# Attention and block-quantised feed-forward layer: the division of the attention sums goes to GpSimd, bias and statistics are rearranged

## The reference

```python
xn = layernorm(x)                       # x: 16 batches x 512 tokens x 128
x  = x + attn(xn) + ffn(xn)
# attn: q = xn@Wqa@Wqb (16 heads of 8), k, v = xn@Wkva@Wkvb (4 heads); rope on q and k;
#       causal softmax(q k^T / sqrt(8)); o = w v; o @ Wout + bout
# ffn:  fp4_linear(silu(fp4_linear(xn, w_gate)) * fp4_linear(xn, w_up), w_down)   # 128 -> 352 -> 128
# fp4_linear quantises both operands in blocks of 16 before the product
```

## Time and profile before

| | us |
|---|---|
| median of 3 runs | 797.62 (795.21 to 798.21) |
| the profiled execution, its own time | 797.94 |
| its span, first to last instruction | 795.9 |
| outside the span | 2.0 |
| one step of the loop, T = 1 to 12 | 44.4 |
| granted TensorE clock, mean | 0.988 |

### The profile page before, as it was taken

The page is one execution under the profiler, slowest core; times in us unless marked ns, Lnnn a source line. Parts: engine busy times, 40 slices in busy tenths (PEclk is TensorE's granted clock), DMA queues, the critical chain, the costliest instruction groups (busy, mean ns, idle before and its releaser), DMA issues.

```text
span 795.9 us, 18365 instructions
## 1 busy us (share of the span) xinstructions
PE 722.8 (91%) x6453; PEld 442.3 (56%) x6453; DVE 644.0 (81%) x1390; ACT 535.1 (67%) x1154; POOL 612.3 (77%) x708
## 2 busy tenths in 40 slices
PE   2467889999999999999999999999999999998986
PEld 1233455665656565665656565565656665665434
DVE  6569788989888888989888988889888988878412
ACT  2213686867777777777776767777776867676672
POOL 5534597878889797878889797878889797856662
PEclk9998899999999999999999999999999999999998
DMA  4423233233334343243334343343434333341111
GB/s 113 115 68 88 73 86 102 86 108 110 96 92 116 104 118 96 89 117 98 103 99 119 88 116 96 91 115 96 108 99 116 87 117 93 93 102 38 56 49 35
DMA packets 85028, 75.48 MB, mean 95 GB/s; under 512 B 28642, under 2 KB 67010, under 8 KB 84938
## 3 DMA queue, kind: packets, MB, share of 16 engines
q1 hardware_dynamic: 84938, 74.32, 34.3%
HBM read 40.45 MB, written 27.25 MB: 85 GB/s over the span
## 4 chain that ended last, share of the span: by engine, by line
PE 39%; POOL 32%; ACT 11%; DVE 7%; issue 6%; DMA 3%; SPq 2%; POOLq 0%; DVEq 0%; ACTq 0%
PE pv_ps L1160 10%; POOL P L554 9%; PE exp_ps L1139 7%; POOL h L564 5%; PE max_ps L1124 5%; ACT P L961 5%; POOL h L567 5%; POOL h L570 4%; PE misc_ps L1184 3%; PE max_ps L1125 3%; PE misc_ps L1192 3%; DVE neg_max L737 3%; PE misc_ps L1209 3%; POOL q_split L645 2%; POOL rstd L596 2%
## 5 line engine op out<-in xcount | busy, mean ns | idle before, releaser
L737 DVE TENSOR_REDUCE neg_max<-max_ps 128x1 f32<-128x512 f32 (+3 forms) x768 | 429.9, 593 | 87.1 <-PE max_ps L1125 85.2
L961 ACT ACTIVATE P<-exp_ps 128x512 f32<-128x512 f32 x512 | 294.9, 599 | 167.7 <-PE exp_ps L1139 166.6
L1139 PE MATMUL exp_ps<-Q,K 128*128 128x512 bf16 (+3 forms) x1024 | 244.0, 301 | 10.3 <-ACT P L961 6.5
L1124 PE MATMUL max_ps<-K,Q 128*128 128x384 bf16 (+2 forms) x768 | 199.2, 278 | 18.9 <-DMA Kd<-K 11.7
L1125 PE MATMUL max_ps<-Kd,Q 128*128 128x128 bf16 x1024 | 191.3, 221 | 2.1 <-DVE neg_max L737 2.0
L554 POOL TENSOR_SCALAR_AFFINE_SELECT P<-P 128x512 f32<-128x512 f32 x256 | 161.8, 667 | 26.8 <-ACT P L964 26.8
L1160 PE MATMUL pv_ps<-P,V 128*32 128x512 f32 (+3 forms) x2048 | 163.9, 438 | 1.9 <-POOL P L554 0.8
L1124 PEld LDWEIGHTS max_ps<-K,Q 128*128 128x128 bf16 x768 | 75.9, 100 | 93.3 <-DVE neg_max L737 47.2
L1125 PEld LDWEIGHTS max_ps<-Kd,Q 128*128 128x128 bf16 x1024 | 98.4, 100 | 46.1 <-issue 22.7
L1139 PEld LDWEIGHTS exp_ps<-Q,K 128*128 128x128 bf16 x1024 | 79.7, 98 | 48.4 <-ACT P L961 27.1
L585 POOL TENSOR_TENSOR h<-gate_sb,up_half 128x352 f32<-128x352 f32 x64 | 59.6, 932 | 58.7 <-DVE gate_sb L750 58.6
(11 more groups left out here) (128 smaller groups left out, 974.1 us busy)
## 6 DMA issues: line engine op xcount, KB each, us to landing
Q<-q_scr SPq DMA_DIRECT2D x64, 224.0 KB
o_scr<-oT SPq DMA_DIRECT2D x31, 256.0 KB, 2.6
q_scr<-q_split SPq DMA_DIRECT2D x16, 384.0 KB, 2.6
Kd<-K SPq DMA_DIRECT2D x64, 96.0 KB
x_in<-x SPq DMA_DIRECT2D x16, 256.0 KB, 4.5
q_scr<-q_split SPq DMA_DIRECT2D x16, 256.0 KB, 2.9
x_res<-x SPq DMA_DIRECT2D x16, 256.0 KB, 5.7
out<-y SPq DMA_DIRECT2D x32, 128.0 KB, 4.3
```

What stands on the lines that cost most here:

```text
L737: nc.vector.tensor_reduce(neg_max[:, pr // 4, heads[0]:heads[0] + len(heads), pr % 4, i], max_ps[r % 3][:, 0:len(heads) * n].rearrange("p ...
L961: nc.scalar.activation(P[g % 2][:, hh + r % 2, col:col + 512], ps[:, :], ACT.Exp, scale=SCALE).then_inc(exp_done, 1)
L1124: nc.tensor.matmul(ps[:, col:col + d], Qt, Kt[:, half, g, 0:d], start=True, stop=True)
L1139: last = nc.tensor.matmul(exp_ps[n % 2][:, col:col + width], K[par][:, half, pr // 2, kb * 128:(kb + 1) * 128], Q[par][:, pr, kb * 128:S], ...
```

## The change

- `normalize` (the product `onT`) is issued by GpSimd, after `split_rest` and in front of `hidden(3)`, and no more by VectorE.
- `var_eps` is made on VectorE between tiles (3,4) and (3,5); `neg_mean` is gone, `shift` is one `scalar_tensor_tensor` on VectorE at the start of slot 5; GpSimd keeps `rstd`.
- v goes from PSUM straight to `V` by two VectorE copies, without `v_stage`; `V` has three buffers instead of two.
- The bias is row 96 of the third piece of `wdT`, against a row of ones in `hqT`; `x_bias` (GpSimd) is gone and y is made with `x_res`. The load of `x_res` for batch T-1 is issued at the start of step T instead of that for batch T.

```diff
-            (bout_sb[:, :], bout.partition_broadcast(128)),
+            (wdT[FC[2][1]:FC[2][1] + 1, 2, :], bout.unsqueeze(0)),
...
 # SP, start of a step
-                if T.has(0):
-                    T.wait(sp, x_bias_done, 1, 0, 0)
-                    sp.dma_start(x_res[:, :, :], x[T.batch(0)]...).then_inc(x_res_loaded, 16)
+                if T.has(-1):
+                    T.prev().misc_wait(sp, misc_read, "out1")
+                    sp.dma_start(x_res[:, :, :], x[T.batch(-1)]...).then_inc(x_res_loaded, 16)
...
 # POOL
-            def statistics(T):
-                T.wait(pool, mv_done, NT, 3, NT)
-                nc.gpsimd.tensor_scalar(var_eps[:, :], bn_mv[:, :, 1], EPS, None, ALU.add).then_inc(var_done, 1)
-                nc.gpsimd.tensor_scalar(neg_mean[:, :], bn_mv[:, :, 0], -1.0, None, ALU.mult).then_inc(var_done, 1)
-                T.wait(pool, var_done, 2, 3, 2)
+            def normalize(T):
+                T.wait(pool, o_loaded, 32, -1, 32)
+                T.wait(pool, o_inv_in, 32, -1, 32)
+                nc.gpsimd.tensor_tensor(onT[:, :], o_raw[:, :], o_spread[:, :], ALU.mult).then_inc(o_normed, 1)
+            def deviation(T):
+                T.wait(pool, var_done, 1, 3, 1)
                 nc.gpsimd.tensor_tensor(rstd[:, :], var_eps[:, :], half_neg[:, :], ALU.pow).then_inc(rstd_done, 1)
-                T.wait(pool, rstd_done, 2, 3, 1)
-                nc.gpsimd.tensor_tensor(shift[:, :], neg_mean[:, :], rstd[:, :], ALU.mult).then_inc(rstd_done, 1)
...
-                    for s in range(2):
-                        nc.gpsimd.tensor_copy(V[T.par(1)][...], v_stage[...]).then_inc(v_ready, 1)
...
-                statistics(T)
+                deviation(T)
                 split_rest(T, 1, 0)
+                normalize(T)
                 hidden(T, 3)
...
-                    nc.gpsimd.tensor_tensor(x_bias[:, :, :], x_res[:, :, :], bout_sb..., ALU.add).then_inc(x_bias_done, 1)
...
 # DVE
-                reduces(3, 4, 5)
+                reduces(3, 4)
+                if T.has(3):
+                    T.wait(dve, mv_done, NT, 3, NT)
+                    T.wait(dve, rstd_done, 2, 2, 1)
+                    nc.vector.tensor_scalar(var_eps[:, :], bn_mv[:, :, 1], EPS, None, ALU.add).then_inc(var_done, 1)
+                reduces(3, 5)
...
-                    nc.vector.tensor_copy(v_stage[:, :, :], misc_ps[1][:, 0:128]...).then_inc(misc_read[1], 1)
+                    for odd in range(2):
+                        nc.vector.tensor_copy(V[T.third(2)][:, :, odd::2, ...], misc_ps[1][:, 0:128]...)
...
-                reduces(5, 0)
-                normalize(T)
-                reduces(5, 1, 2)
+                if T.has(3):
+                    T.wait(dve, rstd_done, 2, 3, 1)
+                    nc.vector.scalar_tensor_tensor(shift[:, :], bn_mv[:, :, 0], -1.0, rstd[:, :], ALU.mult, ALU.mult)
+                reduces(5, 0, 1, 2)
```

More of the change, by code:

```diff
@@ L90, in batch, with third @@
         return self.t0 + off
+    def third(self, off):
+        return (self.t0 + off) % 3
     def wait(self, eng, sem, per, off, k):
@@ L191, in build @@
         Kd = sb("Kd", [128, 2, KVH, S], BF16)
-        V = [sb(f"V{i}", [128, NT, KVH, 32]) for i in range(2)]
+        V = [sb(f"V{i}", [128, NT, KVH, 32]) for i in range(3)]
         P = [sb(f"P{i}", [128, GH, P_WIDTH]) for i in range(2)]
@@ L534, in _ @@
             nc.gpsimd.memset(half_neg[:, :], -0.5).then_inc(consts_set, 1)
-            for i in range(2):
+            for i in range(3):
                 nc.gpsimd.memset(V[i][:, :, :, :], 0.0).then_inc(pool_const, 1)
@@ L539, in _ @@
             nc.gpsimd.memset(m_split[:, :, 64:128], 0.0).then_inc(pool_const, 1)
-            pool.wait_ge(pool_const, 5)
-            for i in range(2):
+            pool.wait_ge(pool_const, 6)
+            for i in range(3):
                 nc.gpsimd.memset(V[i][:, :, 0::2, 2 * D:2 * D + 1], 1.0).then_inc(pool_const, 1)
@@ L663, in iteration @@
                     quantize(T, 0, 3, *hs)
[L664 to L668, removed]
                 if T.has(3):
@@ L768, in invert @@
                 nc.vector.reciprocal(o_inv[:, g, :], o_sum[:, g, :]).then_inc(o_inv_done, 1)
[L770 to L776, removed]
-                    T.prev().misc_wait(dve, misc_filled, "out1")
-                nc.vector.tensor_tensor(onT[:, :], o_raw[:, :], o_spread[:, :], ALU.mult).then_inc(o_normed, 1)
             def output(T, n):
@@ L784, in output @@
                 if n == 0:
-                    T.wait(dve, x_bias_done, 1, -1, 1)
+                    T.wait(dve, x_res_loaded, 16, -1, 16)
                     T.wait(dve, stored, 32, -1, 0)
@@ L790, in output @@
                 nc.vector.tensor_tensor(y[:, c, :], misc_ps[0][:, 0:2 * E].rearrange("p (c e) -> p c e", c=2),
-                                        x_bias[:, c, :], ALU.add).then_inc(misc_read[0], 1)
+                                        x_res[:, c, :], ALU.add).then_inc(misc_read[0], 1)
             def finish(T):
@@ L813, in finish @@
                 T.wait(dve, stored, 32, -1, 0)
-                T.wait(dve, x_bias_done, 1, -1, 1)
+                T.wait(dve, x_res_loaded, 16, -1, 16)
                 for c, ps in enumerate(misc_ps + exp_ps):
                     dve.wait_ge(last_out, c + 1)
-                    nc.vector.tensor_tensor(y[:, c, :], ps[:, 0:E], x_bias[:, c, :], ALU.add).then_inc(last_y, 1)
+                    nc.vector.tensor_tensor(y[:, c, :], ps[:, 0:E], x_res[:, c, :], ALU.add).then_inc(last_y, 1)
             def iteration(T):
@@ L879, in iteration @@
                     T.wait(dve, x_loaded, 16, 3, 16)
-                    T.wait(dve, var_done, 2, 2, 2)
                     for c in range(NT):
@@ L910, in iteration @@
                     store_weights()
-                reduces(5, 0)
-                normalize(T)
-                reduces(5, 1, 2)
+                if T.has(3):
+                    T.wait(dve, rstd_done, 2, 3, 1)
+                    nc.vector.scalar_tensor_tensor(shift[:, :], bn_mv[:, :, 0], -1.0, rstd[:, :],
+                                                   ALU.mult, ALU.mult).then_inc(rstd_done, 1)
+                reduces(5, 0, 1, 2)
                 hidden_max(T, 3)
@@ L936, in iteration @@
                 reduces(7, 3, 4, 5)
+            nc.vector.memset(hqT[FC[2][1]:FC[2][1] + 1, 2, :], 1.0).then_inc(ones_row, 1)
             nc.vector.memset(last_sums[:, :, 0:HALF], 0.0).then_inc(dve_marks, 1)
@@ L1153, in weighted_sums @@
                     if g == 0:
-                        T.wait(pe, v_ready, 2, off, 2)
+                        T.wait(pe, v_ready, 1, off, 1)
+                        T.prev().prev().misc_wait(pe, misc_read, "v")
                 else:
@@ L1159, in weighted_sums @@
                     for j in range(GH):
-                        last = nc.tensor.matmul(pv_ps[32 * j:32 * j + 32, kb * 128:S], V[T.par(off)][:, kb, g, :],
+                        last = nc.tensor.matmul(pv_ps[32 * j:32 * j + 32, kb * 128:S], V[T.third(off)][:, kb, g, :],
                                                 P[g % 2][:, j, P_COL[kb]:P_COL[kb] + width],
```

34 lines of the change are left out of this document (17 added, 17 removed).

## The result

The changed kernel takes **790.12 us** (median of 6 runs, 788.24 to 792.68); the kernel before, beside it on the same chip, 795.8 (6 runs, 795.02 to 798.21). The ratio is 0.9926, interval 0.99 to 0.9953: 5.7 us less. The profiled execution of the changed kernel is the fastest of its six, 788.24 with a span of 785.8; the profiled one of before was with 797.94 at the upper end of its own (span 795.9). So the two traces differ by 10.1 us where the medians differ by 5.7. A later series of the changed kernel gave 791.1. Ratios leave out executions more than 1.5% above the fastest of their kernel; that is one, the 833.24 of experiment 5.

A forecast was written before the change was run, and what follows sets the result against it. A relay between TensorE with ScalarE and GpSimd bounds a middle step. Terms -3.6, -1.0, -2.6 and +1.65 make -5.55, from 797.9 to 792.4, written 792.2 for the median; own range 790.5 to 794.3, wide range 790 to 798.

The forecast's parts named there:

- T = 0: First step: no product there, so it keeps -1.03 from the statistics; TensorE's wait of 1.5 us leaves room.
- T = 13 and 14: GpSimd makes the product before L564 and TensorE no longer waits for onT: -1.3 each.
- T = 15: Late o_spread holds GpSimd's whole queue; L570 ends near 779.1 instead of 776.65: +1.65.
- Slot 7: Middle steps: without x_bias, x_scale falls by 0.61 and part of TensorE's 0.24 stall at tile (7,5) goes: -0.13.
- The run: GpSimd, T = 1 to 12: -1.03 statistics, +0.20 later hidden(3), -0.44 at L564; sum -0.24, taken as -0.17 a step.
- L564's relief: GpSimd's addition of h_mag, no longer beside onT on VectorE, gets shorter by 0.44 or a little less.
- holds GpSimd some 0.1: Before hidden(3): shift, if it waits for the product's end, gets in first and delays GpSimd; bounds 0 and 0.20.
- TensorE then has 0.27 - 0.1 in hand: At hqT0: the 0.27 wait less 0.1 for a late shift leaves TensorE 0.17, as much as GpSimd gains.
- rival D: Middle steps: shift not held, and VectorE 1.3 us lighter lets TensorE start slot 5 tiles earlier; 790.9, chance 0.10.
- A: Middle steps: L564 stays at 3.31 beside another VectorE instruction, product paid in full; step +0.07, 796.7, chance 0.15.
- B: End of slot 3: var_eps held behind q_split, up to 1.2 us; +0.1 to +0.3 a step, 798.3, chance 0.15.
- C: End of slot 3: var_eps held behind q_split, its price on the path, middle 0.8 a step; 805.5, slower, chance 0.10.

The follow-up runs named there:

- experiment 5: Kernel before with the statistics alone changed: var_eps and shift on VectorE, rstd left on GpSimd; 826.57 us, ratio 1.0349.
- number 10: Kernel before with the v copies alone: two VectorE copies from PSUM into a third buffer of V; 796.42 us, ratio 0.9992.
- number 12: The changed kernel once more, unaltered; 791.1 us, ratio 0.9917 against the kernel before.
- (3): Kernel before with the bias alone as a weight row and x_bias gone; 795.14 us, ratio 0.9973.
- (2): Kernel before with only the product onT moved to GpSimd, in front of hidden(3); 803.2 us, ratio 1.0071.
- (11): Changed kernel, all four statistics on GpSimd, var_eps and neg_mean ahead of q_split's third part except in T = -2; 795.3 us, ratio 0.9983.
- Number 8: Changed kernel with the product of T = 15 alone back on VectorE; 788.57 us, ratio 0.9899.
- (6): Changed kernel with var_eps one tile later, behind tile (3,5); 789.85 us, ratio 0.9911.

## Why the prediction came out as it did

Predicted 792.2, measured 790.12: faster as forecast, 2.1 us too high, inside the wide range of 790 to 798 but 0.4 below the forecast's own 790.5 to 794.3. By medians the gain is 5.7 us where the sum gave 5.55. The mechanism, a relay between TensorE and GpSimd in which GpSimd's run sets the step, is borne out. Two steps of the prediction failed: the level that the sum was taken from, and the size of the term for a middle step.

**The level.** The step is "It stands 0.3 above the median of the runs, so I write 792.2". That median was one of three runs, 797.62; with more of them it is 795.8 here and 796.6 to 797.0 in the three other series, and the profiled execution lies some 1 to 2 above. From 795.8 the same sum gives 790.25.

**The sum is right by parts that are not.** By the starts of `hqT0`, in us; the last column takes two other executions, number 10, whose steps are those of before, and number 12, the changed kernel again:

| part | predicted | before to changed | number 10 to 12 |
|---|---|---|---|
| T = 0 | -1.0 | -1.8 | -1.7 |
| T = 1 to 12 | -3.6 | -5.3 | -2.1 |
| T = 13 and 14 | -2.6 | -3.2 | -3.0 |
| T = 15 | +1.65 | +1.3 | +1.4 |
| from there to the end | 0 | -1.1 | +0.1 |
| sum | -5.55 | -10.1 | -5.2 |

- The term that was mis-sized is "12 x (-0.17 - 0.13) = -3.6": an undisturbed step gained 0.41, not 0.30, which makes -4.9.
- Slot 7, -0.13: measured -0.13 by itself (3).
- The run, -0.17: measured -0.27. The product, 1.23, and what left the run, 1.03, were right, and L564's relief too. What failed is "holds GpSimd some 0.1": a held `shift` takes nothing from `hidden(3)`, which starts 1.23 behind the product as if it were alone. Over twelve steps 1.2 us.
- "TensorE then has 0.27 - 0.1 in hand": had TensorE been 0.1 later, its wait for `h` would have ended with 0.17 of GpSimd's gain. It was 0.10 earlier: GpSimd gave 0.27 and a wait of 0.10 is left. I gave the product's departure from VectorE only the 0.18 of the wait; it is worth 0.35 (2), and the held `shift` costs back 0.1 to 0.2 (11). This was rival D's second half; D's first, that `shift` is not held, is wrong. The step is 0.41 shorter where I had 0.30 and D 0.42.
- T = 0: over four kernels with nearly this head it ends between 120.6 and 122.8, which I did not settle.
- T = 13 and 14: the waits for `onT`, 1.24 and 1.29, are gone, and the steps are 1.57 and 1.66 shorter. So "there is no wait for L570 to fall back on" held. In T = 14 `o_sum` lands late, VectorE waits 1.70 and 1.07, and the gain comes all the same.
- T = 15: GpSimd's idle time before the product is 1.42, not 1.9. Number 8 puts the net price of the new order there at 1.0.
- The last stretch had no term. 0.3 of it follows from T = 15's order; the rest, up to 0.75, goes with the granted clock of the last eight matmuls.
- Disturbed steps were in no term. They carry 0.6 us of the first trace of the changed kernel and 3.5 of the second, 2.9 of the 3.3 by which the two spans differ.

That the sum meets the difference of the medians is thus luck: the undisturbed steps, T = 0 and T = 13 and 14 gained 2.2 to 2.7 more than it had in these pairs, and disturbed steps, 2.6 more in number 12 than in number 10, can take as much back.

**The rivals.** A fell at once: L565 is 2.86 in every step. B was right in its mechanism and wrong as a state of every step: `var_eps` passes ahead by 0.27, I had 0.1 to 0.2, and is caught only where `o_sum` is late. Its price when it is caught in every step behind tile (3,5) is 0.05 (6), not the 0.1 to 0.3. Ahead of that tile, where the changed kernel has it, a caught `var_eps` comes with 0.64 for the step, near the 0.8 of C's middle. So C had a price that occurs, but in one to three steps of an execution and not in twelve; the late transfer has a share in the 0.64 that I did not part from it.

By the Trainium skill, SBUF - State Buffer, section "Who interferes with whom", the instruction that issues first has the shared ports for its whole length and the other blocks: "Issue order, not op shape, decides who blocks." The traces agree, with a number for each case: four elements take 0.16 us free and 1.13 behind `q_split`, 0.15 free and 0.67 behind the product; 512 elements take 1.31 behind the last piece of h and 2.82 behind the addition. By size alone none of this would be there, and the loss in number 5 could not be explained.

**Why the edits together gain what none gains alone.** The product on GpSimd costs 0.63 a step, the statistics on VectorE cost 2.3, the bias gives 0.13, the copies nothing; together they give 0.41. The product must leave VectorE so that an earlier GpSimd does not catch it, and the statistics must leave GpSimd to make room for the product. What stays is one held `shift`.

**What stays open.** How far below 43.85 TensorE's own path could go with `shift` on time; steps of 43.54 were seen where the sums' transfer did not disturb, and even there GpSimd's `h` released `hqT0`. No version beats the changed kernel by more than the measurement tells: numbers 6 and 8 are level with it by the medians, though number 8's trace shows 1.0 us. A shorter way for the sums through SP's queue was not tried.

## What to carry to other kernels

Where two engines shut each other out, ask which instruction of the other engine is running when each one comes up, before shortening a run: here an edit that took 1.0 us off a run put the product behind an instruction of 2.85 instead of one of 0.93, and cost 2.3 a step. Price a set of edits also in pairs, since a part that loses alone may be what lets another gain. Anchor the forecast on several runs, not on one execution, and look in the head and in the last steps for what a moved instruction waits for there. A wait that leaves the list may only have become short: compare the start of the instruction with the end of the one that it waits for. Choose bars on the engine that leads at that place, since the end of `h` says little where TensorE comes to it 2 us later.

## What the runs showed of the hardware beyond that

A four-element instruction on VectorE costs 0.15 us or 1.13, by what GpSimd is doing at its start; in number 5 a `shift` caught by an addition took 2.58 (245.44 to 248.02, the addition 245.14 to 247.99). Each held instruction ends a fixed time after the one that held it: `var_eps` and `shift` by 0.02 to 0.03, the product of 512 elements by 0.55, whatever its own row says. So a duration of 1.31 on VectorE and one of 1.26 on GpSimd for the same product are not the same speed: of the 1.31, 0.76 passes until GpSimd's instruction has ended (332.78 to 333.54). `rstd`, a power of four elements on GpSimd, takes 1.01, where `var_eps` and `shift`, four elements too, take 0.24 and 0.20 there.
